# Edge stage of a four-layer graph network: gathered rows added on TensorE by identity products, ReLU read out of PSUM by ScalarE

## What is computed

```python
# layer 0: weighted sum over the edges
out = segment_sum(edge_weight[:, None] * h[src], dst)
# layer 1: the layer of the edge stage
msg_in = concatenate([h[src], h[dst], edge_attr_2])
msgs = maximum(msg_in @ mW1 + mb1, 0) @ mW2 + mb2
agg = segment_sum(msgs, dst) / clip(count, 1)
upd = maximum(concatenate([h, agg]) @ uW1 + ub1, 0) @ uW2 + ub2 + h
out = layernorm(upd) * gamma + beta
# layer 2: weighted sum over the edges of h @ weight, bias, relu
# layer 3, three times: out = segment_sum(h[src] + edge_attr_128, dst) + h, two dense layers with layernorm and gelu
```

## Time and profile before

| | |
|---|---|
| median of three runs | 5099.75 us |
| the profiled execution's own time | 5105.07 us |
| its span | 5103.0 us |
| TensorE busy with products | 4573.1 us (90%) |
| VectorE busy | 3469.8 us (68%) |
| ScalarE busy | 1866.3 us (37%) |
| GpSimd busy | 2095.9 us (41%) |
| mean granted TensorE clock | 0.963 of full speed |

### The profile page before, as it was taken

One profiled execution on the slowest core, in us unless ns is written; L12 is line 12 of the kernel. 1 busy time (PEld: TensorE's weight loads), 2 busy tenths in 40 slices (PEclk: granted clock), 3 DMA queues, 4 the chain that ended last, 5 costly groups with the idle time before them and its releaser, 6 DMA issues.

```text
span 5103.0 us, 115772 instructions
## 1 busy us (share of the span) xinstructions
PE 4573.1 (90%) x36490; PEld 3823.9 (75%) x36490; DVE 3469.8 (68%) x9487; ACT 1866.3 (37%) x4197; POOL 2095.9 (41%) x2575
## 2 busy tenths in 40 slices
PE   1799999999887888888888888888989999999998
PEld 0799999999756778777777877777866666666665
DVE  7899999999566766766766767766644444444444
ACT  2565656565412111111111111111134444444445
POOL 7311111111377776766766776766501111111000
PEclk8899999999998999999999999999989999999999
DMA  6354544445555666666666666666655554554554
GB/s 183 129 223 192 215 200 208 208 198 217 170 132 132 187 192 187 199 185 187 197 185 185 200 185 192 198 194 197 185 194 189 189 198 165 183 185 177 189 189 152
DMA packets 555431, 953.05 MB, mean 187 GB/s; under 512 B 116386, under 2 KB 417554, under 8 KB 523746
## 3 DMA queue, kind: packets, MB, share of 16 engines
q1 hardware_dynamic: 278354, 703.00, 38.0%
q0 software_dynamic: 58304, 121.69, 9.2%
q10 hardware_dynamic: 218448, 124.48, 8.7%
HBM read 695.11 MB, written 253.77 MB: 186 GB/s over the span
## 4 chain that ended last, share of the span: by engine, by line
PE 59%; DVE 17%; issue 8%; POOL 4%; DVEq 4%; ACTq 3%; DMA 3%; ACT 2%; SPq 0%; POOLq 0%
PE ps L1601 22%; PE ps L1301 9%; PE ps L1398 7%; PE ps L1518 4%; PE ps L1285 4%; DVE ACC L2090 4%; PE ps L1287 4%; DVEq L470 3%; PE ps L1387 3%; POOL BIG L861 3%; DVE BIG L1948 3%; ACTq L1051 2%; DVE T L1868 2%; DVE BIG L1954 2%; DVE BIG L1868 2%
## 5 line engine op out<-in xcount | busy, mean ns | idle before, releaser
L861 POOL DMA_INDIRECT BIG<-table,IDX x1664 | 1647.5, 990 | 674.9 <-issue 472.4
L1398 PE MATMUL ps<-BIG 128*128 128x257 f32 x3328 | 961.3, 413 | 58.6 <-DVE ACC L2090 25.7
L2090 DVE TENSOR_TENSOR ACC<-ACC,ps 128x257 f32 x1664 | 701.2, 421 | 373.7 <-DVE ACC L2090 135.6
L1398 PEld LDWEIGHTS ps<-BIG 128*128 128x128 f32 x3328 | 591.9, 202 | 200.4 <-DVE ACC L2090 55.7
L1387 PE MATMUL ps<-T,BIG 128*128 x3328 | 602.8, 304 | 101.2 <-DVE BIG L1941 96.6
L1301 PE MATMUL ps<-H,ACC 128*128 128x128 f32 x4802 | 690.1, 284 | 0.0
L1387 PEld LDWEIGHTS ps<-T,BIG 128*128 128x128 f32 x3328 | 526.2, 195 | 165.1 <-issue 138.6
L1301 PEld LDWEIGHTS ps<-H,ACC 128*128 128x128 f32 x4802 | 588.2, 192 | 0.2 <-ACT ACC L1010 0.2
L1038 ACT ACTIVATE IDX<-SRC 128x4 int32<-128x4 uint16 x416 | 84.7, 204 | 1346.2 <-DVE BIG L1948 1331.8
L1010 ACT ACTIVATE BIG<-ps 128x392 bf16<-128x392 f32 x784 | 390.2, 498 | 468.7 <-PE ps L1287 468.7
L2254 DVE TENSOR_TENSOR NODE<-NODE,ps 128x128 f32<-128x128 f32 x441 | 126.6, 287 | 546.1 <-PE ps L1601 535.9
(11 more groups left out here) (277 smaller groups left out, 8408.9 us busy)
## 6 DMA issues: line engine op xcount, KB each, us to landing
weight_mat<-ACC SPq DMA_DIRECT2D x49, 3136.0 KB, 9.2
REL_WT<-count_mat SPq DMA_DIRECT2D x73, 1568.0 KB, 6.5
BIG<-count_mat SPq DMA_DIRECT2D x72, 1568.0 KB, 6.6
count_mat<-BIG SPq DMA_DIRECT2D x49, 1568.0 KB, 12.8
REL_WT<-weight_mat SPq DMA_DIRECT2D x270, 256.0 KB
BIG<-rel_tab ACTq DMA_DIRECT2D x416, 128.0 KB
BIG<-in_edge_attr SPq DMA_DIRECT2D x832, 64.0 KB
BIG<-in_edge_attr ACTq DMA_DIRECT2D x832, 64.0 KB
```

The lines of the kernel that those rows point to most:

```text
L861: pool.indirect_dma_start(G[:, q * QUAD + u, :], None, tables[1], bass.IndirectOffsetOnAxis(ap=IDX[:, q, u:u + 1], axis=0)).then_inc(gathe ...
L1398: return pe.matmul(PS[4 + u][:, 0:2 * F + 1], D[k * QUAD + u], HE[:, k * QUAD + u, :], start=True, stop=True)
L2090: last = dve.tensor_tensor(to, to, bank_[:, 0:2 * F + 1], ALU.add)
```

## The change

TensorE now waits for the gathered rows ahead of `edge_rows` and adds them in PSUM with a third product per step: the identity matrix times the 128 gathered rows (fp32, 128 columns). VectorE's `rows_plus` is gone, and with it `rows_added`. ScalarE waits for `pre_ps` in its place and takes the ReLU straight from the PSUM bank into `HE`. TensorE may write a bank again once the ReLU of two quads before is done.

```diff
             def act_quad(i, q, more):
-                act.wait_ge(rows_added, i * QUADS + (q + 1))
+                act.wait_ge(pre_ps, i * QUADS + (q + 1))
                 if more:
                     stage(i * U + (q + QUADS) * QUAD, q)
-                hidden = HE[:, q * QUAD:(q + 1) * QUAD, 0:F]
-                act.activation(hidden, hidden, ACT.Relu).then_inc(relu_done, 1)
+                act.wait_ge(slots_free, i * U + (q + 1) * QUAD)
+                act.activation(HE[:, q * QUAD:(q + 1) * QUAD, 0:F], PS[q % 2][:, :].rearrange("p (u f) -> p u f", f=F), ACT.Relu).then_inc(relu_done, 1)
...
             def edge_rows(i, q, b, again_):
                 pe.wait_ge(dt_ready, i * QUADS + (q + 1))
                 pe.wait_ge(a18_in[q], (i + 1) * 16)
+                pe.wait_ge(gathered[q], GATHERED0 + (i + 1) * 16 * QUAD)
                 if again_:
-                    pe.wait_ge(rows_added, i * QUADS + (q - 1))
+                    pe.wait_ge(relu_done, i * QUADS + (q - 1))
                 for u in range(QUAD):
                     to = PS[q % 2][:, u * F:(u + 1) * F]
                     pe.matmul(to, DT[:, q % 2, u * P:(u + 1) * P], T1[:, b[q * QUAD + u], :], start=True, stop=False)
-                    mm = pe.matmul(to, A18[:, q, u * P:(u + 1) * P], w18[:, :], start=False, stop=True)
+                    pe.matmul(to, A18[:, q, u * P:(u + 1) * P], w18[:, :], start=False, stop=False)
+                    mm = pe.matmul(to, ident[:, :], G[:, q * QUAD + u, :], start=False, stop=True)
                 mm.then_inc(pre_ps, 1)
...
-            def rows_plus(i, q):
-
-                k = q % QUADS
-                dve.wait_ge(gathered[k], GATHERED0 + (i + q // QUADS + 1) * 16 * QUAD)
-                dve.wait_ge(pre_ps, i * QUADS + (q + 1))
-                dve.tensor_tensor(HE[:, k * QUAD:(k + 1) * QUAD, 0:F], PS[q % 2][:, :].rearrange("p (u f) -> p u f", f=F), G[:, k * QUAD:(k + 1) * QUAD, :],
-                                  ALU.add).then_inc(rows_added, 1)
```

More of the change, by code:

```diff
@@ L407, in build_gnn @@
         general_gathered = [sem(f"general_gathered{k}") for k in range(SLOTS)]
-        rows_added = sem("gathered_rows_added")
+        pass
         t_std, xr_used = sem("t_std_ready"), sem("x_row_used")
@@ L1964, in dve_quad @@
                     quad_first(i, q, on(1), on(2))
-                if on(1):
-                    rows_plus(i, q - 1)
                 if on(0):
@@ L2183, in edge_way @@
                         quad_first(i, q, n >= 1, n >= 2)
-                    if 1 <= n <= QN:
-                        rows_plus(i, q - 1)
                     if n < QN:
```

## The result

The changed kernel takes 5068.03 us (median of five runs, 5066.81 to 5068.62), the kernel before 5099.12 in the runs beside it: ratio 0.9942, 95% interval 0.9928 to 0.9957. It is 31 us **faster** (0.6%), where 22 us slower was forecast. The profiled executions differ by 36.8 us in span (5103.0 to 5066.2).

What follows compares the result with a forecast made beforehand. GpSimd bounded the first half, VectorE narrowly the second; after the change TensorE would: 1,922 + 12 + 20 + 10 + 5 + 30 = 1,999 us against 1,977, +22, so median 5,122 us, range 5,055 to 5,195.

Steps and rivals of the forecast that it cites:

- What bounds the kernel: Edge stage: GpSimd bounds the 63 quads without layer 2 weight products, VectorE (1,879 us) by a little the 352 with them.
- VectorE loses 211 us, TensorE gets 313: Edge stage's second half: dropping the add leaves VectorE 1,668 us alone; the identity products bring TensorE to 1,922.
- ScalarE's ReLU from PSUM: Edge stage: reading PSUM takes 597 ns against 618, no change; ScalarE's position starts earlier, 2.2 us into TensorE's.
- What TensorE then still loses: Edge stage's second half: TensorE losses kept on top of 1,922 us: body start 20, landings 10, adds 5, clock 30.
- copies: TensorE's waits for ScalarE's PSUM copies in the second half, 124.7 us before, should mostly vanish; 12 us taken.
- start of a body: TensorE's 60.6 us idle ahead of L1387, from late VectorE and its own register reads; 20 us taken to remain.
- landings of edge attributes: TensorE's 21.0 us of waits in the second half; ScalarE issues half a position earlier, so 10 us taken.
- The clock: TensorE's second-half clock of 0.96, 79 us lost, rises to 0.985 with shorter gaps; 30 us taken to remain.
- The upper bound: Second half: 1,922 us plus all present TensorE losses (125, 61, 21, 14, 79) makes 2,222, or +245 us.
- TensorE packs tightly: Rival, second half: TensorE loses under 45 us and the clock nears 1.00; 5,070 us with 25 lost; chance 0.24.
- ScalarE holds TensorE: Rival, second half: even-position hand-overs of PSUM banks wait as before or longer; +135 us, 5,235; chance 0.12.
- nearly free products: Rival, second half: TensorE takes the added products beside its waits, GpSimd bounds at 1,816; -161 us, 4,940; chance 0.04.

Runs made afterwards that it cites:

- both adds: Kernel before with the identity product added and VectorE's add kept, so gathered rows count double: 5124.32 us, ratio 1.0047.
- the doubled product: Changed kernel with the identity product done twice, so gathered rows count double: 5378.07 us.
- the mixes: Changed kernel with some quads' rows added by VectorE as before, the rest by TensorE; those tabled with losses of 28 to 35 us took 4,977 to 5,008 us.
- one in four: Changed kernel with the second quad of each body added by VectorE, the other three by TensorE: 5005.94 us, ratio 0.9819; 0.975 in a slow run.
- two in four: Changed kernel with every odd quad added by VectorE, the rest by TensorE: 4976.78 us, ratio 0.9759; 1.0226 in a slow run.
- five in eight: Changed kernel with quads 0, 1, 3, 5 and 7 of every eight added by VectorE: 5888.53 and 5840.18 us, ratios 1.0173 and 1.0167.

## Why the prediction was wrong

- **What bounds the kernel**: GpSimd in the first half fits: it took 328.8 us before and 331.8 with the change, and 327.9 to 335.1 in all kernels of this speed, with TensorE's work there from none to two products a step more. That VectorE bounded the second is only half right: its own 1,879 us were 96 short of the pace.
- **VectorE loses 211 us, TensorE gets 313** and needs 1,922: right. The pitch is 0.555 us a step, and the second product cost 306 us; VectorE's busy time fell by 197 us (1,381 to 1,185).
- **ScalarE's ReLU from PSUM**: 597 ns forecast, 581 in the median. Its earlier start was forecast rightly too: at 2.2 us behind the start of `edge_rows`, with the ReLU at 2.53 us in the trace, and the waits for its copies fell from 124.7 us to 0.6.
- **The step that failed is "What TensorE then still loses"**, 77 us with ScalarE's 12. Measured, 13: copies 0.6 for 12; start of a body 7.9 (5.9 + 1.1 + 0.9) for 20; landings of edge attributes 0 for 10; VectorE's adds 0 for 5; the clock reads 1.00, so less than half a per cent for 30 us. I had taken each gap of the engine that was *not* the bound and let a part of it stand when it became the bound. But a gap there is first of all that engine's spare time: the longer position filled it, and VectorE and ScalarE, freed from the add, were early. What looked like a cause of its own was TensorE's register read:

```profile
L470 PEldq TENSOR_LOAD <-body_tab x88: 1856/1970/3017, 1703.0 to 3615.5; - x88
...
2494.85 1.05 PE L1520 MATMUL ps<-T,NODE 128*128 128x128 f32 x8
2495.84 0.48 PE L1388 MATMUL ps<-T,BIG 128*128 x2
```

  The 88 reads last 184 us in all, and TensorE idles 7.9 us ahead of L1388, because products that were handed out before a read go on beside it. The read that starts at 2493.33 and lasts 2.14 us is done at 2495.47, while the weight products run to the next `edge_rows` at 2495.84. So the length of the read is not its price.

- **The upper bound** was worse still: 2,222 us added all of the gaps to TensorE's work. The kernel with both adds, which has the same TensorE work and ScalarE late again, has 1,988.
- **The rivals**: "TensorE packs tightly" is what happened, at the point named (losses under 45 us), with the reasons given for it. It got 0.24 because I took the 88 register reads as evidence against it without looking at when they start. "ScalarE holds TensorE" fell with the 0.6 us of waits in the changed kernel. The nearly free products fell with the doubled product.
- **The clock**: VectorE's long register reads had opened gaps like that of the earlier trace rows; I left 30 of their 79 us standing though I had also found 254 us of room on VectorE. By the same argument there was nothing to open them.
- **The signs** listed for "right" all appeared (pitch, vanished waits, VectorE waiting 362 us where it waited 154, clock of the span 0.983). They did not tell the forecast from its rival: all of them are also signs of the tight packing.
- **The range** of 5,055 to 5,195 holds 5,068 only because it had been drawn to take in that rival; the forecast itself had the direction wrong.

## What to carry to other kernels

Give each engine its own time from pitches and counts, and take the largest as the estimate once the change has put one engine clearly ahead (by over 5% here): the second half came out 13 us over 1,922, and 11 over 1,816. Don't add the present gaps of an engine that is about to become the bound; they are its spare time, and they fill, as long as the engines it waits for come early: with VectorE's add kept, 66 us stayed. Where two engines lie within a few per cent, add a loss: 28 to 35 us in 1,900 for the mixes, 66 for both adds. Before reading a run that holds an engine back, measure in its trace how late the engine became; and when the moved work can be split by item, try a split.

## What the runs showed of the hardware

- TensorE's clock went from 0.96 to 1.00 in the same stretch when its products stood close together, and 24% more products (14,541 for 11,728) ran in it in less time. The 0.04 x 1,975 = 79 us that the lower clock took before were no loss to come on top once TensorE set the pace.
- TensorE's reads of registers from HBM take 1.97 us in the median and run beside products already handed out: 184 us of them for 7.9 us of idle time.
- The same kernels can be 10 to 19% slower, and their order changes then. Where the kernel before takes 5,750 to 5,798 us, one in four is at 0.975 of it, two in four at 1.0226 and five in eight at 1.017, where two in four is at 0.9759 beside 5,102 us. It is not shown to be a property of a chip: the record gives chip number 10 for 5,102 us and, twelve minutes later, for 5,798. The slower traces lose nothing behind the edge stage (1,430 to 1,434 us from the last `edge_rows`, against 1,427 to 1,434), about 50 us ahead of it, and the rest in it (second half of two in four: 2,647 us for 1,845). A gather lasts as long in either (955 and 958 ns in the median, two in four). VectorE and ScalarE have waits there that the profile puts down to `remote`, no instruction of this core, and that no other trace has. Within 1900:3500 of two in four:

```profile
DVE ACC L2104 <- remote: 246.0, 62, 7.3
```

What is slower in these runs was not found. A version that balances engines closely should be timed more than once, beside the kernel before each time.
